# Differential attention with routed experts: a lead of 23 steps, products among the first scores, the last norm in the experts' block

## What is computed

```python
A1 = einsum('bhqd,bhkd->bhqk', Q1, K1) * scaling      # 16 heads, 2048 x 2048
A2 = einsum('bhqd,bhkd->bhqk', Q2, K2) * scaling
attn = softmax(A1) - lamb * softmax(A2)
out = layernorm(einsum('bhqk,bhkd->bhqd', attn, V) @ Wo) * gamma + beta
x = layernorm(x + out)
# experts: top-2 of 8, softmax of the two logits as weights
for e in range(8):
    h = gelu(layernorm(x, ln_g[e], ln_b[e]) @ w1[e] + b1[e])      # exact gelu
    ffn = ffn + combine[..., e] * (h @ w2[e] + b2[e])
x = layernorm(x + ffn)
```

## Time and profile before

| what | value |
|---|---|
| time, median of 3 runs | 3319.23 us (3314.82 to 3320.06) |
| the profiled execution | time 3325.93 us, span 3324.2 us |
| busy: PE, DVE, ACT, POOL | 3127.3, 2795.0, 2541.0, 440.3 us |
| projection | 0 to 183.6 us |
| attention | to 2602.0 us |
| join, route | to 2757.5 us |
| experts | to 3296.5 us |
| finish | to 3324.1 us |

### The profile page before, as it was taken

How to read it: one execution, slowest core, us unless ns; L and a number is a source line. 1 busy time by engine, 2 the same in 40 slices (tenths; PEclk the granted TensorE clock), 3 DMA queues, 4 the chain that set the end, 5 groups by cost and what they waited for, 6 DMA issues and landing times. The chain is left out here.

```text
span 3324.2 us, 84031 instructions
## 1 busy us (share of the span) xinstructions
PE 3127.3 (94%) x29395; PEld 1446.7 (44%) x29396; DVE 2795.0 (84%) x2957; ACT 2541.0 (76%) x4691; POOL 440.3 (13%) x637
## 2 busy tenths in 40 slices
PE   8989999999999999999999999999999867999995
PEld 4423332333333333333333333333333656999994
DVE  3589999999999999999999999999999884433343
ACT  3359998998999899899989998999999532333333
POOL 3000000000000000000000000000000443555544
PEclk9989999999999999999999999999999978999997
DMA  6620101011010101111010101011010661222224
GB/s 168 154 47 9 28 21 28 21 31 28 9 30 21 28 9 28 40 25 28 21 28 12 28 21 28 18 34 28 9 30 21 225 237 26 36 38 35 38 36 121
DMA packets 100989, 151.45 MB, mean 46 GB/s; under 512 B 21808, under 2 KB 66728, under 8 KB 98828
## 3 DMA queue, kind: packets, MB, share of 16 engines
q1 hardware_dynamic: 84684, 127.43, 15.3%
q0 software_dynamic: 15904, 18.66, 3.6%
HBM read 85.74 MB, written 60.30 MB: 44 GB/s over the span
## 5 line engine op out<-in xcount | busy, mean ns | idle before, releaser
L707 DVE TENSOR_REDUCE half_max<-scores 128x2 f32<-128x1024 f32 x2064 | 2351.9, 1212 | 56.2 <-PE scores L613 51.8
L681 ACT ACTIVATE probs<-bank 128x512 f32<-128x512 f32 x4104 | 2227.1, 594 | 158.8 <-PE bank L629 91.1
L661 PE MATMUL bank<-probs,V 128*32 128x256 f32 x16384 | 1323.1, 395 | 66.1 <-ACT probs L681 39.2
L613 PE MATMUL scores<-K,Q 48*128 48x512 f16 x4128 | 814.4, 391 | 12.9 <-DVE half_max L707 8.0
L629 PE MATMUL bank<-Q,K 50*128 50x512 f16 x4104 | 796.7, 382 | 0.3 <-ACT probs L681 0.3
L661 PEld LDWEIGHTS bank<-probs,V 128*32 128x32 f32 x16384 | 323.7, 108 | 628.3 <-issue 542.8
L613 PEld LDWEIGHTS scores<-K,Q 48*128 48x128 f16 x4128 | 198.1, 93 | 891.6 <-DVE half_max L707 705.2
L629 PEld LDWEIGHTS bank<-Q,K 50*128 50x128 f16 x4104 | 375.7, 94 | 112.5 <-ACT probs L681 5.0
L583 POOL TENSOR_SCALAR max_parts<-row_max 128x16 f16<-128x16 f32 x65 | 16.5, 254 | 2119.0 <-DVE row_max L713 2119.0
L1517 ACT ACTIVATE h<-u 128x1024 f32<-128x1024 f32 x71 | 75.0, 1057 | 270.0 <-DVE u L1553 270.0
L1481 PE MATMUL pre<-xgT,w 128*128 128x128 f32 x2272 | 267.2, 276 | 4.3 <-ACT xgT L1511 4.2
(11 more groups left out here) (188 smaller groups left out, 1128.7 us busy)
## 6 DMA issues: line engine op xcount, KB each, us to landing
attended<-att SPq DMA_DIRECT2D x64, 256.0 KB, 2.5
W<-in_L_ffn_w_dram SPq DMA_DIRECT2D x16, 1024.0 KB, 6.9
heads<-attended SPq DMA_DIRECT2D x7, 2048.0 KB, 9.4
Q<-q_parts SPq DMA_DIRECT2D x102, 128.0 KB, 5.6
K<-k_parts SPq DMA_DIRECT2D x102, 128.0 KB, 6.0
q_parts<-parts SPq DMA_DIRECT2D x64, 128.0 KB, 2.4
k_parts<-parts SPq DMA_DIRECT2D x64, 128.0 KB, 2.8
xs<-in_L_attn_x_dram SPq DMA_DIRECT2D x8, 512.0 KB, 4.6
```

The source lines that it names most:

```text
L613: mm = nc.tensor.matmul(scores[:, b, h, :], Q[p][r, c, up, t * P:(t + 1) * P], K[p][r, up, kc * TC:(kc + 1) * TC], start=True, stop=True)
L661: mm = nc.tensor.matmul(banks[att_bank[s // KB]][32 * u:32 * u + 32, q], V[wp][:, wk, u // 2, :], probs[:, 4 * s % RING + u, q], start=(wk ...
L681: nc.scalar.activation(probs[:, i % RING, :], banks[tile_bank[i]][:], ACT.Exp, scale=SCALE).then_inc(exp_done, 1)
L707: nc.vector.tensor_reduce(half_max[lc % 2][:, :, up, t, kc], scores[:, b], AX.X, ALU.max).then_inc(max_done[b], 1)
```

## The change

Three edits.

1. `AHEAD` goes from 24 to 23. So `CUT` goes from 8 to 9: the maxima are taken and turned one step later in each chunk, while PE still wants them at step 14. Ahead of the loop there are 7 leading items (14 score pairs) in place of 8, and the eight transposed products stand between the score pairs of the last two of them, two behind each, in place of behind all.
2. In the experts `pre` becomes two buffers, PE waits for `u_ready` of the tile before the last, and ACT norms tile 1 before the gelu of tile 0.
3. The finish becomes the tail of the experts' block, in the same instruction queues, with no barrier between. Its `z` and output tiles lie in the space of `W1`. Its one memset on POOL stands at the head of the experts.

```diff
-    stage_finish(nc, locals())
...
-    AHEAD = KB + 6 + LAG
+    AHEAD = KB + 5 + LAG
...
-            pe.wait_ge(max_loaded[0], MXD + 1)
-            for ls in range(LAG):
-                for u in range(UNITS):
-                    scores_of(0, ls, u)
+            for i in range(PRE, AHEAD):
+                for b in range(2):
+                    score_pair(i, i // KB, i % KB * 2 + b)
+                    if i >= AHEAD - LAG:
+                        if i == AHEAD - LAG and b == 0:
+                            pe.wait_ge(max_loaded[0], MXD + 1)
+                        for u in range(2 * b, 2 * b + 2):
+                            scores_of(0, i - (AHEAD - LAG), u)
...
-        pre = ps("pre", [P, IC, P], F32)
+        pre = [ps(f"pre{i}", [P, IC, P], F32) for i in range(2)]
...
+        retired = W1[:].rearrange("p e k i -> p (e k i)")
+        z = retired[:, 0:ROWS].rearrange("p (n j d) -> p n j d", n=NC, j=FT)
...
             sp.wait_ge(added, 16 * USED)
+            for n in range(NC):
+                sp.dma_start(z[:, n], x1d[0:T].rearrange("(p n j) d -> n p j d", p=P, n=NC)[n]).then_inc(z_loaded[n], 16)
...
+            nc.gpsimd.memset(minus_half[:], -0.5).then_inc(half_set, 1)
+            pool.wait_ge(half_set, 1)
             take_routes(0, 0)
...
                 if left >= 1:
-                    pe.wait_ge(u_ready, n + 1)
+                    if not isinstance(n, int) or n > 0:
+                        pe.wait_ge(u_ready, n)
                     times_w1(n + 1, 1 - p)
...
             norm_rows(0, 0)
+            norm_rows(1, 1)
             gelu(0, 0)
-            norm_rows(1, 1)
             run(act, step)
```

More of the change, by code:

```diff
@@ L615, in score_pair @@
                 mm.then_inc(scores_ready[b], 1)
-            for i in range(PRE, AHEAD):
-                for b in range(2):
-                    score_pair(i, i // KB, i % KB * 2 + b)
             def scores_of(base, ls, u, attended=None):
@@ L1381, in stage_experts @@
     KD, IC, D, E, I, USED, ident = (a[n] for n in ("KD", "IC", "D", "E", "I", "USED", "ident"))
+    out, NT, T = (a[n] for n in ("out", "NT", "T"))
     GB = 8
@@ L1384, in stage_experts @@
     FAR = XB - 1
+    FT = TPC
+    NC = NT // FT
+    FD = 1
+    FA = FT - FD
     with ExitStack() as ctx:
@@ L1404, in stage_experts @@
         part_loaded = [sem(f"e_part_loaded{i}") for i in range(XB)]
+        retired = W1[:].rearrange("p e k i -> p (e k i)")
+        ROWS = NC * FT * D
+        assert 2 * ROWS <= E * KD * I
+        z = retired[:, 0:ROWS].rearrange("p (n j d) -> p n j d", n=NC, j=FT)
+        fin = retired[:, ROWS:2 * ROWS].rearrange("p (n j d) -> p n j d", n=NC, j=FT)
+        st, mv = sb("f_st", [P, NT, 6], F32), sb("f_mv", [P, NT, 2], F32)
+        ve, rs = sb("f_ve", [P, NC, FT], F32), sb("f_rs", [P, NC, FT], F32)
+        minus_half = sb("f_minus_half", [P, FT], F32)
+        mr, nb = sb("f_mr", [P, NC, FT], F32), sb("f_nb", [P, NC, FT], F32)
+        half_set, st_ready, var_ready, ve_ready, rs_ready, mr_ready, nb_ready, fin_dve, fin_act, gate_f_pool, gate_f_dve = (
+            sem("f_" + n) for n in ("half_set", "st_ready", "var_ready", "ve_ready", "rs_ready", "mr_ready", "nb_ready",
+                                    "fin_dve", "fin_act", "gate_pool", "gate_dve"))
+        z_loaded = [sem(f"f_z_loaded{n}") for n in range(NC)]
+        stored = sem("f_stored")
         block = ctx.enter_context(nc.Block())
@@ L1426, in _ @@
             sp.wait_ge(added, 16 * USED)
+            for n in range(NC):
+                sp.dma_start(z[:, n], x1d[0:T].rearrange("(p n j) d -> n p j d", p=P, n=NC)[n]).then_inc(z_loaded[n], 16)
+            for n in range(NC):
+                sp.wait_ge(fin_dve, FD * (n + 1))
+                sp.wait_ge(fin_act, FA * (n + 1))
+                sp.dma_start(out.rearrange("b (c j p) d -> (b c) p j d", j=FT, p=P)[n], fin[:, n]).then_inc(stored, 16)
+            sp.wait_ge(stored, 16 * NC)
         @block.gpsimd
@@ L1466, in _ @@
             run(pool, step)
+            for n in range(NC):
+                pool.wait_ge(var_ready, FT * (n + 1))
+                pool.sem_inc(gate_f_pool, 1)
+                nc.gpsimd.tensor_scalar(ve[:, n], mv[:, n * FT:(n + 1) * FT, 1], EPS, None, ALU.add).then_inc(ve_ready, 1)
+                pool.wait_ge(ve_ready, n + 1)
+                nc.gpsimd.tensor_tensor(rs[:, n], ve[:, n], minus_half[:], ALU.pow).then_inc(rs_ready, 1)
+                pool.wait_ge(rs_ready, n + 1)
+                nc.gpsimd.tensor_tensor(mr[:, n], mv[:, n * FT:(n + 1) * FT, 0], rs[:, n], ALU.mult).then_inc(mr_ready, 1)
+                pool.wait_ge(mr_ready, n + 1)
+                nc.gpsimd.tensor_scalar(nb[:, n], mr[:, n], -1.0, None, ALU.mult).then_inc(nb_ready, 1)
         @block.tensor
@@ L1480, in times_w1 @@
                     for k in range(KD):
[L1481 removed]
+                        mm = nc.tensor.matmul(pre[p][:, c, :], w1[p][:, k, c * P:(c + 1) * P],
                                               xgT[p][:, k * P:(k + 1) * P], start=(k == 0), stop=(k == KD - 1))
@@ L1534, in _ @@
             norm_rows(0, 0)
+            norm_rows(1, 1)
             gelu(0, 0)
-            norm_rows(1, 1)
             run(act, step)
-        @block.vector
-        def _(dve):
-            def take_w1(n, p, used):
-                e = owner(dve, n)
-                if used is not None:
-                    dve.wait_ge(pre_ready, used)
-                nc.vector.tensor_copy(w1[p][:], W1[:, bass.ds(e, 1), :, :].rearrange("p o k i -> p (o k) i")
-                                      ).then_inc(w1_ready, 1)
[L1548 to L1556, removed]
-                p = q % 2
-                if left >= 2:
-                    take_w1(n + 2, p, n + 1)
-                if left >= 1:
-                    add_b1(n + 1, n + 1)
-                e = owner(dve, n)
-                dve.wait_ge(ys_ready, n + 1)
-                dve.wait_ge(py_ready, n + 1)
-                nc.vector.tensor_tensor(y[p][:], py[p][:, 0:D], b2s[:, bass.ds(e, 1), :].rearrange("p o d -> p (o d)"),
-                                        ALU.add).then_inc(y_ready, 1)
-            take_w1(0, 0, None)
-            take_w1(1, 1, None)
-            add_b1(0, None)
-            run(dve, step)
@@ L1574, in stage_finish @@
[L1574 to L1622, removed]
@@ L1632, in _, with take_w1, add_b1, step @@
         def _(dve):
+            def take_w1(n, p, used):
+                e = owner(dve, n)
+                if used is not None:
+                    dve.wait_ge(pre_ready, used)
+                nc.vector.tensor_copy(w1[p][:], W1[:, bass.ds(e, 1), :, :].rearrange("p o k i -> p (o k) i")
+                                      ).then_inc(w1_ready, 1)
+            def add_b1(n, p, used):
+                e = owner(dve, n)
+                if used is not None:
+                    dve.wait_ge(h_ready, used)
+                dve.wait_ge(pre_ready, n + 1)
+                nc.vector.tensor_tensor(u[:], pre[p][:], b1c[:, bass.ds(e, 1), :].rearrange("p o c -> p c o")
+                                        .to_broadcast((P, IC, P)), ALU.add).then_inc(u_ready, 1)
+            def step(n, it, q, left):
+                p = q % 2
+                if left >= 2:
+                    take_w1(n + 2, p, n + 1)
+                if left >= 1:
+                    add_b1(n + 1, 1 - p, n + 1)
+                e = owner(dve, n)
+                dve.wait_ge(ys_ready, n + 1)
+                dve.wait_ge(py_ready, n + 1)
+                nc.vector.tensor_tensor(y[p][:], py[p][:, 0:D], b2s[:, bass.ds(e, 1), :].rearrange("p o d -> p (o d)"),
+                                        ALU.add).then_inc(y_ready, 1)
+            take_w1(0, 0, None)
+            take_w1(1, 1, None)
+            add_b1(0, 0, None)
+            run(dve, step)
             def moments(n):
@@ L1637, in moments @@
                 dve.wait_ge(st_ready, FT * (n + 1))
-                dve.sem_inc(gate_dve, 1)
+                dve.sem_inc(gate_f_dve, 1)
                 for j in range(FT):
```

## The result

The changed kernel takes 3309.51 us (median of 18 runs, 3303.66 to 3317.37), the kernel before 3317.99 us in the same session (18 runs, 3312.56 to 3324.99). The ratio is 0.9976, 95% interval 0.9969 to 0.9983: 8.0 us gained (5.6 to 10.3), where 12.8 and a median of 3306.4 us were forecast. The profiled executions differ by more, spans of 3324.2 and 3308.3 us, since that of the kernel before lies 8 us above its median.

| stage | before | after |
|---|---|---|
| projection | 183.6 | 183.7 |
| attention | 2418.4 | 2407.5 |
| join, route | 155.5 | 155.5 |
| experts' start to the issue of `z` | 539.0 | 531.8 |
| `z` issued to SP at the last barrier | 27.3 | 27.3 |

The account below looks back on a forecast made before the run. DVE's reduction of the leading scores was taken to bound attention, PE the experts, so gains lie at seams: -6.1 - 1.75 - 4.9 = -12.8 us, 3313.1 us for the profiled execution, median 3306.4 us, range 3300 to 3315.

Parts of the forecast that it names:

- (b): Head of attention: PE's clock rises no earlier than before; gain 9.4 us, to 3309.8 us; chance 0.12.
- (c): End of the program: POOL's drain moves there from ahead of the finish; gain 9.1 us, to 3310.1 us; chance 0.12.
- the signs that were named: Trace: first loop reduction near 202.2 us, two to four at 1.98, chunks of 36.6 us, no long last POOL drain.
- Term 1: Head of attention: first loop reduction 5.25 us earlier, plus 0.85 us from the clock; 6.1 us gained.
- Its far end: Head of attention: no slow half step and no pause of DVE, 9.6 us gained.
- Term 1, the clock: Start of the attention loop: three slow half steps in place of four, 0.85 us gained.
- The maxima: Their way over DRAM in each attention chunk: slack falls from 4.2 to 1.9 us, at no cost.
- Rival (e): Attention chunks: maxima come too late for PE, every microsecond costs 64, at the far end 3454 us; chance 0.03.
- Term 2: Head of the experts: products of tile 1 start 1.95 us earlier; 1.75 us gained with the memset's delay.
- Term 3: Ahead of the finish: loads of `z` no longer wait for POOL's drain at the barrier; 4.9 us gained.
- its other end: End of the program: the drain is owed there, 3.7 us behind SP, leaving 1.2 us of gain.
- rival (d): Seams, mostly the loop's seven repeats: PE's clock phase eats 6.0 us of the gain, giving 3315.8 us; chance 0.07.

Follow-up runs that it names:

- e_pre: The kernel before with only the second `pre` buffer and the norm of tile 1 ahead of gelu: 3316.30 us, ratio 0.9999.
- e_join: The kernel before with only the finish joined to the experts' block: 3318.43 us, ratio 0.9998.
- e_rest: The changed kernel with the old `stage_attend`, so only the `pre` buffers and the joined finish are new: 3312.85 us, ratio 0.9988.
- e_again: The changed kernel itself, measured once more: 3309.55 us, ratio 0.9976 to the kernel before.
- e_drain: The changed kernel with one more POOL drain right behind its last indirect DMA: 3307.42 us, ratio 0.9969 to the kernel before.
- e_head: The kernel before with only the new `stage_attend` (lead 23, products among the last leading scores): 3315.20 us, ratio 0.9994.
- e_head2: The kernel before with only the new `stage_attend`, the same program measured a second time: 3317.15 us, ratio 0.9995.
- e_lead22: The changed kernel with a lead of 22 in place of 23: 3306.84 us, ratio 0.9967 to the kernel before.
- e_inter: The kernel before with the transposed products between the last leading score pairs, lead still 24: 3319.01 us, ratio 0.9993.
- e_lead21: The changed kernel with a lead of 21 in place of 23: 3505.08 us in its one run.

## Why the prediction was right, and where not

The time lies in the range, and faster was the likelier side. The gain was forecast at 12.8 us and is 8.0, and the median lies 3.1 us above the one forecast, at the times of rivals (b) and (c), 3309.8 and 3310.1. Of the signs that were named, the long POOL drain that ends last was to be absent and is there, and one slow reduction came instead of two to four.

**Term 1, first reduction.** Forecast 202.17 us, gain 5.25; measured 202.36, and 5.2 us from the barrier on (23.7 to 23.9 in four profiled executions with the old order, 18.5 to 18.7 in five with the new one and a lead of 23). The chain of score pair, exp and `weigh` held. Its far end took the pause of DVE as 0.9 us; by the same rows it is 1.2 (DVE is free at 203.22 less two reductions, 200.96, and goes on at 202.17), and 1.25 was measured.

**Term 1, the clock.** Three slow half steps were forecast against four; one came. But the four of the earlier trace rows were no property of the order. With the same attention code four, one, four and two reductions wait (the kernel before, e_pre, e_join, e_rest), and with the new order one, three, two, two, two (the change, e_again, e_drain, e_head, e_head2). The means are 2.75 and 2.0, so this part is 0.6 us on average, and 2.6 in the profiled pair. A step that failed is the reading of one execution as the rule; the size came out near by luck.

**The maxima.** Slack was forecast at 1.9 us. From e_lead22 PE wants them 3.9 us behind the turn there (263.35 to 267.28), a step of 2.29 us more in the change; there the turn is at 263.88 and the reads land near 268.0 (an estimate: issued at 266.08, 1.9 us under way as in e_lead22), so 2.1 us. The cost was nothing, as taken. Rival (e) did not happen, but its mechanism is real two steps on, at 1.5 times the price that it gave a late microsecond.

**Term 2.** Forecast 1.95 (1.75 with the memset taken off), measured 2.0 in the groups of e_pre, e_rest and the change. The table load was followed by gelu at once, 2762.09 behind 2760.80 + 1.28, with its input written since 2760.96: the further drain that the Trainium skill ("ScalarE: Activation LUTs", What ACT_TABLE_LOAD costs) adds is not in this row, where the engine did have work behind the load. The measurement decides.

**Term 3.** This is the other step that failed, and the larger one by the sum. The 4.9 us ahead of the finish came, but "its other end", the drain owed at the end of the program, came too, at 2.3 us of its 3.7: the term is 2.6. The argument against rival (c), that 30 us lie between the last indirect DMA and the new end, did not hold: the drain took 7.24 us there in every kernel of this form that was not drained before, and 0.36 in e_drain. Terms 2 and 3 are seen in every trace: from the experts' start to the issue of `z` it takes 538.9 to 542.3 us in four executions with neither edit (the kernel before, e_head, e_head2, e_inter) and 531.7 to 532.8 in eight with both.

**The sum.** By the traces 5.2 + 0.6 + 2.0 + 2.6 = 10.4 us, by the ratio 8.0 (5.6 to 10.3). Of the 4.8 us that the forecast was too high, 2.3 are the drain's; the other 2.4 are placed nowhere, and the interval nearly covers them. Nor do the times of the parts add up: the three edits alone give 2.8 us by ratios, edit 1 alone (1.8) and edits 2 and 3 together (4.0) give 5.8, the change 8.0. Each of these has an uncertainty of 2 to 4 us, so the ratios do not say in which edit something is lacking.

Edit 1 is clear in the traces once the loop is set aside. From the first to the last turned maximum of the loop it takes 2342.6 to 2351.4 us in those nine executions, 2346.8 in the mean with the old order and 2347.5 with the new. The rest of attention, its head and its end, takes 64.2 to 67.0 us in the four with the old order and 59.3 to 60.8 in the five with the new: 5.9 us less in the mean, which is term 1 as measured. DVE's wait for PE from 225 us on does not grow (41.4 us with the new order against 41.0 in the mean), so rival (d) is not seen. The profiled pair is apart by 3.2 us in the loop as well, and by 2.6 instead of 0.6 us in slow reductions; that is scatter of the two executions.

The granted clock that is on record for each run tells more than the medians. Most of the scatter goes with it: over the 88 runs of the kernel before in the three sessions, 0.001 of clock goes with 2.8 us. The mean times, us (runs), at equal clock:

| granted clock | before | the change (both calls) | edit 1 alone (both calls) | edits 2 and 3 |
|---|---|---|---|---|
| 0.971 | 3320.1 (37) | 3315.1 (5) | 3317.6 (4) | 3316.2 (2) |
| 0.972 | 3317.6 (25) | 3311.9 (5) | 3315.8 (8) | 3314.6 (2) |
| 0.973 | 3313.9 (9) | 3309.1 (8) | 3314.1 (4) | 3311.6 (2) |

At equal clock the change is 4.8 to 5.7 us faster, edits 2 and 3 are 2.3 to 3.9, and edit 1 alone is between 0.2 us slower and 2.5 us faster. The other 3 us of the 8.0 go with the clock itself, 0.9725 in the mean of the change's 29 runs against 0.9714. Part of that is edit 1's own doing, since it takes time at half clock away at the head; how much is not shown. Why edit 1 alone gives so little in its times, with 5.9 us in its traces, is open.

## What to carry to other kernels

Moving work across a barrier moves what the barrier collected. Look up which engine's drain is long, and place that drain explicitly where the engine has nothing to do. A single profile says what a step costs, but not how often a clock-dependent one occurs: before a count of slow steps enters a sum, see it in several executions. Where gains are of the size of the scatter, compare runs at equal granted clock. Before a lead is shortened, measure the way that it covers (here 2.0 us for the write and 1.9 for the reads), and stay at the last lead that covers it: from a lead of 22 to one of 21 the time rose by 6%.

## What the runs showed of the hardware

- POOL's drain at the end of a block was 8.7 us directly behind its indirect DMAs and still 7.24 us 26 us after the last of them was issued (3274.86, drain at 3300.8). Drained once, the next takes 0.36 us.
- A pause of PE of 2 us, with PE busy for 7.9 of the 8 us ahead of it at a granted clock of 1.00, was followed by half clock (1.2 GHz) for 3.5 us (e_lead21). In 64 chunks this lowered the mean granted clock from 0.973 to 0.950.
- The projection, the same code everywhere, took 183.2 to 187.7 us. In the long cases the clock fell in the middle of it, to 0.66 from 40 to 50 us in e_head (187.1 us) and e_pre (187.7). That is not all that sets its length, as e_again had 0.83 there and took 183.2 us. e_head, then the change, the same stretch:

```profile
40.00:50.00 10.00, 7.72 (x15) 3.36 (x14) 3.45 (x5) 4.39 (x8) 2.34 (x1) 0.66 0.83 206
```

```profile
40.00:50.00 10.00, 7.80 (x22) 3.70 (x20) 4.83 (x7) 5.38 (x10) 2.34 (x1) 1.00 0.88 194
```

PE is busy as long in both, at 0.66 and at 1.00 of the clock, and does 15 matmuls in place of 22. Differences of this size between two executions tell nothing of an edit.
